# Normalised rows written inside the lag attention, and the order of loads at the start of the routing

## What is computed

```
x = x + tanh(g_xattn[0]) * autocorrelation(layernorm(x), ctx, ctx)      # L0: 8 heads, 11 best lags by FFT
x = x + tanh(g_ffn[0])   * experts(layernorm(x))                        # L0: 16 experts, 2 per row
x = x + tanh(g_xattn[1]) * attention(layernorm(x), ctx, Wq,bq, Wk,bk)   # L1
x = x + tanh(g_ffn[1])   * quantised_swiglu(layernorm(x))               # L1
```

```
probs = softmax(x @ gate_w.T);  vals, idx = top_k(probs, 2);  vals /= sum(vals)
h = silu(x @ g_e.T) * (x @ u_e.T)          # per chosen expert e
out = sum over the two of  val_e * (h @ d_e.T)
```

## Time and profile before

| | |
|---|---|
| runs | 1598.67, 1599.94, 1595.01 us; median 1598.67 |
| profiled execution | 1598.1 us, its span 1596.4 us |
| TensorE | busy 1360.1 us, 85% |
| VectorE | busy 797.0 us, 50% |
| ScalarE | busy 523.3 us, 33% |
| GpSimd | busy 428.1 us, 27% |

### The profile page before, as it was taken

One profiled execution on the slowest core, in us unless ns is written; L12 is line 12 of the kernel. 1 busy time (PEld: TensorE's weight loads), 2 busy tenths in 40 slices (PEclk: granted clock), 3 DMA queues, 4 the chain that ended last, 5 costly groups with the idle time before them and its releaser, 6 DMA issues. The chain is left out here.

```text
span 1596.4 us, 19695 instructions
## 1 busy us (share of the span) xinstructions
PE 1360.1 (85%) x6035; PEld 894.1 (56%) x6041; DVE 797.0 (50%) x2181; ACT 523.3 (33%) x827; POOL 428.1 (27%) x481
## 2 busy tenths in 40 slices
PE   5999999999996799898888788259999999927886
PEld 2454454454452674346666576158888888714443
DVE  3678778778774444002122122265444442227996
ACT  2322322322320420004344344322222222148884
POOL 1223223223222002502111112361111100035885
PEclk9999999999997868999899999679999999968999
DMA  4210210400200623005667665433332321060111
GB/s 178 79 54 27 79 53 26 171 13 14 93 1 0 226 94 104 15 0 184 191 209 234 207 216 184 156 92 118 106 101 87 101 67 53 27 217 27 53 53 79
DMA packets 53378, 159.14 MB, mean 100 GB/s; under 512 B 7120, under 2 KB 15312, under 8 KB 53200
## 3 DMA queue, kind: packets, MB, share of 16 engines
q1 hardware_dynamic: 41792, 120.20, 21.4%
q0 software_dynamic: 11536, 38.30, 8.1%
HBM read 112.82 MB, written 45.66 MB: 99 GB/s over the span
## 5 line engine op out<-in xcount | busy, mean ns | idle before, releaser
L44 PE MATMUL xa_bank<-xa_xT_hi,M_hi 128*128 128x256 f32 x512 | 153.7, 300 | 0.0
L46 PE MATMUL xa_bank<-xa_xT_hi,M_lo 128*128 128x256 f32 x512 | 144.2, 282 | 0.0
L45 PE MATMUL xa_bank<-xa_xT_lo,M_hi 128*128 128x256 f32 x512 | 144.2, 282 | 0.0
L52 PE MATMUL la_bank<-la_v_raw,la_tab 128*128 128x512 f32 x256 | 118.5, 606 | 29.5 <-ACT la_v_spec L285 16.3
L1026 PEld LDWEIGHTS ex_bank<-ex_gu,ex_xT 128*128 128x128 f32 x624 | 119.6, 194 | 22.4 <-issue 20.9
L52 PE MATMUL la_bank<-la_osum,la_tab 128*128 128x512 f32 x256 | 117.4, 613 | 13.8 <-POOL la_osum L246 13.8
L1026 PE MATMUL ex_bank<-ex_gu,ex_xT 128*128 128x224 f32 x624 | 127.3, 358 | 0.7 <-ACT ex_xT L961 0.7
L246 POOL TENSOR_TENSOR la_osum<-la_oprod 128x512 f32<-128x512 f32 x64 | 82.7, 1313 | 153.4 <-DVE la_oprod L405 153.4
L52 PE MATMUL la_bank<-la_wT,la_tab 128*128 128x512 f32 x256 | 112.6, 592 | 1.2 <-ACT la_wT L306 1.2
L52 PEld LDWEIGHTS la_bank<-la_v_raw,la_tab 128*128 128x128 f32 x256 | 48.0, 192 | 96.1 <-issue 55.8
L1212 ACT ACTIVATE xa_A<-xa_bank,shift 128x256 f32<-128x256 f32 x64 | 30.3, 473 | 209.7 <-PE xa_bank L46 209.7
(11 more groups left out here) (264 smaller groups left out, 2684.5 us busy)
## 6 DMA issues: line engine op xcount, KB each, us to landing
produced<-ex_y SPq DMA_DIRECT2D x39, 512.0 KB, 3.0
ex_gu<-in_gate_up SPq DMA_DIRECT2D x16, 896.0 KB, 6.2
X<-in_x SPq DMA_DIRECT2D x8, 1024.0 KB, 7.1
la_v_raw<-in_ctx SPq DMA_DIRECT2D x16, 512.0 KB, 4.3
produced<-la_zeros SPq DMA_DIRECT2D x16, 512.0 KB, 5.2
normal<-rt_xn SPq DMA_DIRECT2D x16, 512.0 KB, 3.6
xa_fT<-in_ctx_T SPq DMA_DIRECT2D x8, 1024.0 KB, 5.6
xa_f<-in_ctx SPq DMA_DIRECT2D x8, 1024.0 KB, 5.0
```

The costliest lines, as they stand in the source:

```text
L44: pe.matmul(out, a[0], b[0], start=first, stop=False)
L45: pe.matmul(out, a[0], b[1], start=False, stop=False)
L46: return pe.matmul(out, a[1], b[0], start=False, stop=last)
L52: return pe.matmul(out, a, b, start=first, stop=last)
```

## The change

Two things move. The normalised rows that the experts gather are no longer those of the routing's ring. ScalarE makes them a second time within the lag attention, batch by batch, two tiles at once into a buffer of their own (`rows`), and stores them itself with one DMA of 1 MB. This stands in its step between the query normalisation and the copy of the weights, one batch per two steps; the last batch's comes after the loop, and ScalarE waits for its landing before it leaves the stage. The routing keeps its ring for the turns, but stores nothing. In SyncE's program of the routing, Wq goes up to second place, behind the router weights and ahead of the two bias rows.

```diff
+        rows = sb("rows", [P, 2, D])
...
         def _(act):
             act.wait_ge(s["gate_in"], 16)
+            act.nop().then_inc(s["rows_out"], 16)
...
+            def rows_out(b):
+
+                act.wait_ge(scales_after.ready, b + 1)
+                at_least(act, s["rows_out"], 16 * b + 16)
+                for j in range(2):
+                    tile = 2 * b + j
+                    act.activation(rows[:, j, :], X[:, bass.ds(tile, 1), :].rearrange("p o d -> p (o d)"), ACT.Identity,
+                                   scale=scales_after.scale[:, bass.ds(tile, 1)],
+                                   bias=scales_after.shift[:, bass.ds(tile, 1)]).then_inc(s["rows_made"], 1)
+                act.wait_ge(s["rows_made"], 2 * b + 2)
+                act.dma_start(normal[bass.ds(2 * b * P, 2 * P), :].rearrange("(j p) d -> p j d", p=P), rows[:]).then_inc(s["rows_out"], 16)
...
                         normalise(*next2, j)
+                earlier = on(-2)
+                if earlier and earlier[2] == 1:
+                    rows_out(earlier[1])
                 if now:
                     weights_out(now[0])
             steps(act, step)
+            rows_out(B - 1)
+            act.wait_ge(s["rows_out"], 16 * B + 16)
...
             sp.dma_start(gw[:], gate_wT.rearrange("(k p) e -> p k e", p=P)).then_inc(s["gw_in"], 16)
+            sp.dma_start(W[1][:], Wq.rearrange("(k p) n -> p k n", p=P)).then_inc(s["wq_in"], 16)
             sp.dma_start(b_raw[:, 0, :], bq).then_inc(s["b_in"], 16)
             sp.dma_start(b_raw[:, 1, :], bk).then_inc(s["b_in"], 16)
...
-            for t in range(TILES):
-                if t == TILES // 2:
-                    sp.dma_start(W[1][:], Wq.rearrange("(k p) n -> p k n", p=P)).then_inc(s["wq_in"], 16)
-                sp.wait_ge(s["xn_ready"], t + 1)
-                sp.dma_start(normal[t * P:(t + 1) * P, :], xn[:, t % RING, :]).then_inc(stored[t % RING], 16)
-            for i in range(RING):
-                sp.wait_ge(stored[i], 16 * (TILES // RING))
+            sp.wait_ge(s["b_in"], 32)
+            sp.wait_ge(s["wq_in"], 16)
...
                     act.wait_ge(s["turned"], t - RING + 1)
-                    act.wait_ge(stored[t % RING], 16 * (t // RING))
```

More of the change, by code:

```diff
@@ L93, with lag_attention @@
 TABLE_COLS = 2 * 4 * P * 2 + 2 * L + 4 * L
-def lag_attention(nc, x, ctx, gate, tables, Wk, Wk_home, X, scales_after, produced):
+def lag_attention(nc, x, ctx, gate, tables, Wk, Wk_home, X, scales_after, produced, normal):
     C = 512
@@ L151, in lag_attention @@
                    corr_pe corr_sb maxed exed wdone wdone2 wtr wt_ready wspec
-                   oprods osums out_pe top_chain pchain achain tgd""".split()
+                   oprods osums out_pe top_chain pchain achain tgd rows_made rows_out""".split()
         s = {n: sem(n) for n in names}
@@ L604, in merged_product, with route @@
     return last
-def route(nc, gate_wT, X, norm, normal, token_of, token, place, slots, weights, first_tile, Wq, W, M32, bq, bk,
+def route(nc, gate_wT, X, norm, token_of, token, place, slots, weights, first_tile, Wq, W, M32, bq, bk,
           shift, key_bias, constant):
@@ L653, in route @@
         s = {n: sem(n) for n in names}
-        stored = [sem(f"stored{i}") for i in range(RING)]
         block = ctx.enter_context(nc.Block())
@@ L1698, in build @@
             M_hi, Wk_home = with_guest("M_hi", "Wk")
-            lag_attention(nc, x, ctx, g_xattn, tables, Wk, Wk_home, X, running, produced)
+            lag_attention(nc, x, ctx, g_xattn, tables, Wk, Wk_home, X, running, produced, normal)
             M_lo, M32 = with_guest("M_lo", "M32")
@@ L1707, in build @@
                 W = [Wk_home, lists.enter_context(nc.sbuf_tensor("Wq", [P, KD, D], F32))]
-                route(nc, router_T, X, running, normal, token_of, token, place, slots, weights, first_tile, Wq, W, M32, bq, bk,
+                route(nc, router_T, X, running, token_of, token, place, slots, weights, first_tile, Wq, W, M32, bq, bk,
                       shift, key_bias, constant)
```

## The result

The changed kernel took 1627.15 us in the median of four runs (1622.47 to 1645.01), the kernel before 1596.84 beside it (1592.98 to 1599.94). A fifth run of the changed kernel, 1636.42 us, enters the ratio but not the median. The ratio is 1.0219, 95% interval 1.0148 to 1.029. The kernel is slower, by 30 us in the medians and by 35 in the ratio; forecast was 1632. Medians in this document are of all runs; ratios leave out runs at a visibly lower mean clock than the others of the same kernel.

A forecast was written before the change was run, and what follows sets the result against it. In the routing, TensorE was taken as occupied nearly throughout, a good part at half clock. Terms 7.5 - 4.0 + 10.4 + 19.7 = 33.6 us, on 1598.1, gave 1631.7, against the median 1632; 8-in-10 range 1599 to 1643.

The forecast's parts named there:

- Row work within the lag attention: Lag attention, batches 0 to 6: 2.9 us of ScalarE work a batch fits in 5.25 us of idle, cost 0.
- The fear of 20 us without the cover: Lag attention: without idle time ahead of the weight copy, up to 2.9 us a batch, 20 us over seven.
- Batch 7's tail: End of lag attention: normalisations, issue and landing of 1 MB before the barrier, unhidden, cost 7.5 us, bounds 6.7 and 9.6.
- Ring: Routing: stores out of the ring go, and with them TensorE's wait behind them, minus 4.0 us.
- second rival: Routing: bias rows land by about 534 despite Wq, no standstill, rounds at full clock; 1589, faster; chance 0.10.
- Bias rows behind Wq: Start of routing: bias rows land with Wq or later, VectorE and TensorE wait; delay 10.4 us, bounds 8.0 and 12.9.
- The clock: Routing: after standing TensorE restarts at 0.50, all 14 rounds at half, ten more than before, 19.7 us.
- The rival in which the clock comes back: Routing: TensorE needs 3.4 us at half after restart, then runs at full; 1601, bounds 1597 to 1606; chance 0.13.
- the prediction's condition: Routing: TensorE stands about ten microseconds after its 16 turns and begins again at 0.50.
- The rival that the bias rows don't wait: Same as the second rival: small loads pass between pieces of Wq, no standstill; 1589, chance 0.10.

The follow-up runs named there:

- e9: e5's kernel with four more normalisations of 128x1024 behind the two of each of batches 0 to 6, into an unread buffer: 1581.16 us, ratio 0.9887.
- e7: e1's program run again beside e8, the changed kernel with both bias rows ahead of Wq: 1593.6 us, ratio 0.9961.
- e8: e5's program run again beside e7, bias rows first and batch 7's tiles stored from the routing's ring: 1584.67 us, ratio 0.9897.
- e5: e1's kernel with batch 7's two tiles stored by SyncE from the routing's ring instead of by ScalarE: 1580.47 us, ratio 0.9915.
- e6: Kernel before with Wq issued ahead of the store of tile 12 instead of tile 8: 1584.53 us, ratio 0.9921.
- e1: Changed kernel with the two bias rows issued ahead of Wq instead of behind it: 1587.59 us, ratio 0.9902.
- e4: Changed kernel with eleven unread 128x512 products on TensorE between the sixteen turns and the rounds: 1593.4 us, ratio 0.9973.
- e2: Kernel before with Wq alone moved to second place, ring stores kept in the routing: 1618.43 us, ratio 1.0127.

## Why the prediction was right

*Row work within the lag attention: 0.* Right. The idle time ahead of the weight copy went from 5.26 to 3.00 us on these steps, with the issue of 0.39 us within the 3.00, and e9 shows that even three times the work is covered. The fear of 20 us without the cover used too small a cover.

*Batch 7's tail: 7.5 (6.7 to 9.6).* Measured 6.6 in the trace, 7.6 between e7 and e8. The 1 MB store landed in 4.0 us; I had taken 5.0 from a 1 MB load, and the lower bound, 4.2, was still above it, so 6.6 lies just under the range. (The terms listed, 2.3, 0.1 and 5.0, add up to 7.4.)

*Ring: -4.0, counted together with ten rounds at half clock.* The wait is gone. In the sum of the changed kernel -4.0 is right, because the rounds behind it run at half clock anyway. By itself the wait was worth more, 13.8 us in the traces of e5 and e6: the 4 us, and the clock that was lost with them. The prediction priced this in its second rival: merge 41.2 us after the stage start; e1, e5 and e6 showed 42.9, since the clock fell in the last rounds, where I had put it full (in e4 it held).

*Bias rows behind Wq: +10.4 (8.0 to 12.9).* The mechanism held in every step: issue order, landing with Wq, VectorE's wait, TensorE standing. The size is 9.3: TensorE began its pairs 15.03 us after the stage start (538.25 to 553.28), before 5.68 (529.12 to 534.8). I had put the rows 1.2 us behind Wq, from the program's start. They came 0.3 behind it.

*The clock: +19.7.* The size is right, and on this term the answer hung. All 14 rounds took 4.26 to 4.27 us. The rival in which the clock comes back is refuted by the 66.52 us at 0.50 in the changed kernel, the 66.53 in e2 and the 66.20 in e7. The Trainium skill's page "TensorE: Matmul & The Clock Gate", section "What's actually happening", has activity release the throttle; the trace disagrees for these pairs, which TensorE worked on for 66.52 of 66.60 us at 0.50. The reason is right for the changed kernel, whose profile shows the clock rise with the turns and fall in the standstill. It is not the whole: in e2 the turns had not raised it, and e7 ran at half clock without a standstill. There the prediction's condition would not have held, and the 19.7 us would have been paid all the same.

*Sum.* Tail 6.6 and merge 24.9 give 31.5 against 33.6 forecast (7.5 + 26.1); 30.3 was measured in the medians, 35 in the ratio. The terms that were off are the tail with the store's landing (0.9) and the bias rows' (1.1), both put too high.

*The rival that the bias rows don't wait* is refuted by the 12.3 us. Its price, 1589, is near what e1 and e7 measured when the rows were put in front: 1587.59 and 1593.6. Part of that is luck: the merge gained 13.8 us and not 15.5 and 1.7 more, and the tail cost 6.6 and not 7.5.

## What to carry to other kernels

In a queue put the small load that someone waits for ahead of the large one that nobody needs yet: the place of one line decided between 1627 and 1590 us here. Look at what stands in program order behind a wait, on the waiting engine, and at which clock the work restarts; here a standstill of 9 us cost 9 us, and the 14 rounds at half clock behind it 27.6 more. A stage's work is best moved where its cover is, but the last batch has none: leave that one where it was.

## What the runs showed of the hardware that I had not expected

Light work can hold a full clock and still not win it. Pairs of a 128x128 turn and a 128x16 product ran at 1.00 for 32.6 us in e5 and in e6, and the same pairs at 0.50 for 66 us in the profiles of the changed kernel, e2 and e7. In the last 4.5 us of e5, nearly all of it logit products alone, the clock was 0.66; in e4 the last rounds held 1.00 up to the merge.

Sixteen or seventeen turns back to back do not raise the clock each time. It rose with their end in the changed kernel and e5, only among the first pairs in e1 (0.50 up to 541.2, the turns over at 540.3), and not at all in e2 and e7, with the same turns.

A copy that waits 5 us for another engine can have more than 5 us of slack: in e9 it came 2.2 us late and the step after made it up.
